# Attention of two layers: another order of score units, row units, value products and transposes

## The reference, cut to what matters

```python
scores = jnp.einsum('bqhd,bkhd->bhqk', q, k) * scale
mask = jnp.tril(jnp.ones((n, n), bool))
scores = jnp.where(mask, scores, -jnp.inf)
attn = jax.nn.softmax(scores, axis=-1)
out = jnp.einsum('bhqk,bkhd->bqhd', attn, v).reshape(b, n, d)
```

## Time and profile before

| | us |
|---|---|
| median of 3 runs (lowest, highest) | 1048.63 (1046.24, 1048.93) |
| profiled execution, own time | 1044.79 |
| its span, first to last instruction | 1043.1 |
| mean granted PE clock | 0.837 |
| busy: PE, DVE, ACT, POOL | 862.9, 605.0, 459.4, 288.2 |
| l0 attention, first row matmul to last copy | 306.3 to 471.3 |
| l1 attention, the same | 747.9 to 913.4 |

### The profile page before, as it was taken

How to read it: one execution, slowest core, us unless ns; L and a number is a source line. 1 busy time by engine, 2 the same in 40 slices (tenths; PEclk the granted TensorE clock), 3 DMA queues, 4 the chain that set the end, 5 groups by cost and what they waited for, 6 DMA issues and landing times. The chain is left out here.

```text
span 1043.1 us, 22638 instructions
## 1 busy us (share of the span) xinstructions
PE 862.9 (83%) x8503; PEld 611.2 (59%) x8503; DVE 605.0 (58%) x2052; ACT 459.4 (44%) x1082; POOL 288.2 (28%) x538
## 2 busy tenths in 40 slices
PE   6874914899968999998999889969889999987884
PEld 3542913777746666657886345534466666576462
DVE  1874695465547878746343634450278878475264
ACT  2573511000003666663232876463246766655054
POOL 0770311355532333330001300000023333340635
PEclk9996556655557999999788999878879999998788
DMA  5055453513210263002000000000000000092461
GB/s 124 1 116 115 123 176 119 108 38 81 55 37 2 50 177 63 2 2 91 1 1 23 6 0 1 1 0 1 1 1 2 2 3 2 2 237 84 173 255 49
DMA packets 54437, 60.48 MB, mean 58 GB/s; under 512 B 9050, under 2 KB 40248, under 8 KB 54073
## 3 DMA queue, kind: packets, MB, share of 16 engines
q1 hardware_dynamic: 43976, 44.31, 15.8%
q10 hardware_dynamic: 7488, 6.85, 2.5%
q0 software_dynamic: 2864, 7.89, 2.2%
HBM read 29.75 MB, written 25.99 MB: 53 GB/s over the span
## 5 line engine op out<-in xcount | busy, mean ns | idle before, releaser
L837 DVE CUSTOM_DVE_ANT_0 l_masked_scores<-psum,mask_q_rows 128x128 bf16<-128x128 f32 (+3 forms) x512 | 220.0, 488 | 60.2 <-PE psum L776 60.2
L854 ACT ACTIVATE l_probs<-psum 128x512 f32<-128x512 f32 (+1 forms) x384 | 171.7, 530 | 75.9 <-PE psum L762 75.8
L868 POOL TENSOR_SCALAR_AFFINE_SELECT l_probs<-l_probs 128x256 f32<-128x256 f32 x256 | 101.5, 409 | 358.1 <-ACT l_probs L854 352.8
L776 PE MATMUL psum<-kb_heads,q_heads 32*128 32x384 f32 (+3 forms) x512 | 93.5, 488 | 10.4 <-DVE l_neg_max_rows L828 8.7
L776 PE MATMUL psum<-l_k_heads,l_q_heads 32*128 32x384 f32 (+3 forms) x512 | 93.8, 492 | 4.4 <-DVE l_neg_max_rows L828 2.7
L762 PE MATMUL psum<-l_q_and_max,l_k_heads 32*128 32x384 f32 (+3 forms) x512 | 91.6, 462 | 0.0
L762 PE MATMUL psum<-l_q_and_max,kb_heads 32*128 32x384 f32 (+3 forms) x512 | 90.9, 457 | 0.0
L796 PE MATMUL psum<-l_probs,rows_32k 128*32 128x256 f32 (+1 forms) x1536 | 82.5, 347 | 1.1 <-POOL l_probs L868 1.1
L776 PEld LDWEIGHTS psum<-kb_heads,q_heads 32*128 32x128 f32 x512 | 58.9, 197 | 18.0 <-DVE l_neg_max_rows L828 8.9
L641 POOL TENSOR_TENSOR v_new_and_ones<-v_and_k_rows 32x128 f32<-32x128 f32 x128 | 54.9, 446 | 49.1 <-DVE v_and_k_rows L618 45.5
L776 PEld LDWEIGHTS psum<-l_k_heads,l_q_heads 32*128 32x128 f32 x512 | 59.5, 198 | 12.0 <-DVE l_neg_max_rows L837 3.9
(11 more groups left out here) (351 smaller groups left out, 1684.7 us busy)
## 6 DMA issues: line engine op xcount, KB each, us to landing
sorted_scratch<-l1p_zeros SPq DMA_DIRECT2D x23, 257.0 KB, 7.1
gram_scratch<-rows_32k SPq DMA_DIRECT2D x4, 1024.0 KB, 5.2
rows_32k<-v_new_and_ones SPq DMA_DIRECT2D x64, 64.0 KB, 2.6
x_rows<-in_L_attn_x_dram SPq DMA_DIRECT2D x16, 128.0 KB, 6.7
heads_scratch<-rows_32k SPq DMA_DIRECT2D x2, 1024.0 KB, 5.4
heads_scratch<-q_kb_T SPq DMA_DIRECT2D x2, 1024.0 KB, 6.0
inverse_scratch<-block_inv SPq DMA_DIRECT2D x2, 1024.0 KB, 4.0
q_heads<-heads_scratch SPq DMA_DIRECT2D x2, 1024.0 KB, 7.0
```

Of the source, the lines that this page charges most:

```text
L776: mm = nc.tensor.matmul(ps[:, row_bank(G, u, i), o:o + w], QT(b, gq)[r, t * P:(t + 1) * P], KT(b, gq)[r, 0:w], start=True, stop=True)
L837: last = nc.vector.tensor_tensor_reduce(out=junk[:, n % 4, o:o + w], in0=ps[:, row_bank(G, u, i), o:o + w], in1=g.maskq[:, N - w:N], scale ...
L854: nc.scalar.activation(PT[:, G % 2, 2 * (u % 2) + i, o:o + w], ps[:, e_bank(G, u, i), 0:w], ACT.Exp, scale=SCALE).then_inc(x_ok, 1)
L868: last = nc.gpsimd.affine_select(out=d, in_=d, pattern=[[0, 2], [1, P]], compare_op=ALU.is_ge, fill=0.0, base=0, channel_multiplier=-1)
```

## The change

Three tables of order change, and all that counts by position in them. Nothing is computed otherwise, and no instruction is added or taken away.

```diff
-PV_TURNS = [(1, 0, 256), (3, 256, 512)]
+SCORE_ORDER = [4, 3, 2, 5, 0, 1]
+ROW_SEQ = [2, 5, 4, 1, 0, 3]
+PV_TURNS = [(2, 0, 256), (5, 256, 512)]
 LEAD = 9
 MAXT_AT = 3
-PV_NEEDS = [max(u for u in range(UNITS) for kb, _ in KEYS[u // 2] if kb * P < q1) + 1 for _, q0, q1 in PV_TURNS]
+SCORE_POS = {u: i for i, u in enumerate(SCORE_ORDER)}
+PV_NEEDS = [max(SCORE_POS[u] for u in range(UNITS) for kb, _ in KEYS[u // 2] if kb * P < q1) + 1 for _, q0, q1 in PV_TURNS]
...
-    return [(n // UNITS, n % UNITS)] if n < UNITS * NGRP else []
+    return [(n // UNITS, ROW_SEQ[n % UNITS])] if n < UNITS * NGRP else []
...
-            SCORE_AT[_G, _k, _i] = len(SCORE_AT)
+            SCORE_AT[_G, SCORE_ORDER[_k], _i] = len(SCORE_AT)
...
-                pe.wait_ge(row_ok, max(ROW_AT[G, UNITS, 0] - 3, ROW_AT[G, UNITS - 1, 1] + 1))
+                pe.wait_ge(row_ok, max(ROW_AT[G, UNITS, 0] - 3, ROW_AT[G, ROW_SEQ[-1], 1] + 1))
...
-                    step([(G, k)], row_unit(LEAD + UNITS * G + k))
+                    step([(G, SCORE_ORDER[k])], row_unit(LEAD + UNITS * G + k))
...
-                    act.wait_ge(e_ps, 2 * UNITS * G + 2 * u + i + 1)
-                    if u == 0 and i == 0 and G >= 2:
+                    act.wait_ge(e_ps, 2 * UNITS * G + 2 * SCORE_POS[u] + i + 1)
+                    if u == SCORE_ORDER[0] and i == 0 and G >= 2:
...
-                for u in range(UNITS):
+                for u in SCORE_ORDER:
```

More of the change, by code:

```diff
@@ L674 @@
 PT_AT = [0, 512, 1024, 896]
-PV_TURNS = [(1, 0, 256), (3, 256, 512)]
+SCORE_ORDER = [4, 3, 2, 5, 0, 1]
+ROW_SEQ = [2, 5, 4, 1, 0, 3]
+PV_TURNS = [(2, 0, 256), (5, 256, 512)]
 LEAD = 9
 MAXT_AT = 3
-PV_NEEDS = [max(u for u in range(UNITS) for kb, _ in KEYS[u // 2] if kb * P < q1) + 1 for _, q0, q1 in PV_TURNS]
+SCORE_POS = {u: i for i, u in enumerate(SCORE_ORDER)}
+PV_NEEDS = [max(SCORE_POS[u] for u in range(UNITS) for kb, _ in KEYS[u // 2] if kb * P < q1) + 1 for _, q0, q1 in PV_TURNS]
 def row_unit(n):
-    return [(n // UNITS, n % UNITS)] if n < UNITS * NGRP else []
-SCORE_AT, ROW_AT, UNIT_AT = {}, {}, {}
+    return [(n // UNITS, ROW_SEQ[n % UNITS])] if n < UNITS * NGRP else []
+SCORE_AT, ROW_AT = {}, {}
 for _n in range(LEAD):
     for _i in range(2):
-        ROW_AT[_n // UNITS, _n % UNITS, _i] = len(ROW_AT)
+        ROW_AT[_n // UNITS, ROW_SEQ[_n % UNITS], _i] = len(ROW_AT)
     if _n == UNITS - 1:
@@ L755, in scoresT @@
                         pe.wait_ge(x_ok, SCORE_AT[G, u, i] - 3)
-                    if u == 0 and i == 0:
+                    if u == SCORE_ORDER[0] and i == 0:
                         pe.wait_ge(row_ok, ROW_AT[G, UNITS, 0] + 1)
@@ L770, in rows @@
                         pe.wait_ge(row_ok, ROW_AT[G, u, i] - 3)
-                    if streamed and u == 0 and i == 0 and gq == 0:
+                    if streamed and u == ROW_SEQ[0] and i == 0 and gq == 0:
                         pe.wait_ge(g.heads_ld[b], 16 * (5 if b else 6))
```

## The result

| | before | after |
|---|---|---|
| median, first comparison (4 and 4 runs) | 1047.43 | 1020.8 (1015.75 to 1023.54) |
| ratio and 95% interval | | 0.976 (0.972 to 0.980) |
| median, second comparison, another chip (17 and 6 runs) | 1043.97 | 1017.67 |
| ratio and 95% interval | | 0.973 (0.968 to 0.977) |
| profiled execution, span | 1044.79, 1043.1 | 1020.33, 1018.6 |

The forecast was 1020.2. Here are the stages of the profile after that answer to the earlier trace rows: the lead to maxT(0), to maxT(1), to maxT(2), the 13 turns, and the tail of layer 0; then one turn, which answers to the earlier trace rows; last the 13 turns of layer 1. The columns are those of the earlier trace rows, and behind PEclk stand the DMA share and GB/s.

The account below looks back on a forecast made before the run. No engine is full; the order of waits in a closed PE and DVE loop sets the 9.27 us turn. Each phase gains 13 x 0.94 + 2.0 = 14.2, both 28.4, from 1048.63 to 1020.2 us; 8-in-10 range 1012 to 1031.

Parts of the forecast that it names:

- The turn: One steady loop turn of the attention, from step A to the next A: 8.33 us, 0.94 less than 9.27.
- The added switch: On PE, one more switch between kinds of matmul in each turn, costed at 0.20 us.
- maxT's wait: PE's wait for DVE before maxT in each turn: 0.11 us instead of 0.71.
- The chain: What sets the 8.33 us turn: A, B up to R0, DVE's R0 and R3, maxT, E, F, pv1.
- pv0's cover: pv0's wait for all six units is hidden by 2.5 us of pv1 and steps A to C.
- Ends of a phase: Start and tail of each attention: 2.0 us gained at the start (bounds 0 and 3), 0 at the tail.
- The sum: Both attentions: 13 x 0.94 + 2.0 = 14.2 us gained in each, 28.4 together, so 1020.2 on the runs' scale.
- Rival 1: PE's busy time is real, so a turn gains at most 0.51 us; time 1033; chance 0.09.
- the rule: Trainium skill page: matmul busy time is no measure of headroom, weight-load busy time is better; it names DVE here (81%).
- Rival 2: No wait left: PE's 7.92 us sets the turn; time 1010; chance 0.04.
- Rival 3: Nothing won: a wait on the critical chain (pv1's exp or R4's bank) returns in full; time 1048; chance 0.04.
- Rival 4: Slower: PE at 1.2 GHz in part of the steady loop; 1058 with 6 such turns; chance 0.04.

Follow-up runs that it names:

- split_maxT: Changed kernel, but only maxT's fourth transpose waits for R3 half 1, the three others go when the bank is free; 1017.27 us, 8.36 a turn.
- short_reads: Changed kernel, but DVE reads only 256 of the 512 columns of R0 and R3; 1009.43 us in a single run, 8.36 a turn.
- pool_4us: Changed kernel with eight extra memsets on POOL in front of the masks of S1 in each group; 1102.42 us, 10.32 a turn.
- turns_only: Kernel before with only the value products moved (pv0 behind the third step, pv1 behind the sixth), old unit orders; 1061.76 us, 9.82 a turn.
- short_both: Changed kernel with R0 and R3 reads cut to 256 columns, and QM too from the third group on; 1013.93 us, 8.28 a turn.
- orders_only: Kernel before with the new orders of score and row units, value products left where they were; 1098.43 us, 10.78 a turn.

## Why the prediction was right

- **The turn.** 8.36 for 8.33, and every station of the turn within 0.03. The terms were durations of the trace of before at the same clock, and the two waits that decide (R3 half 1 on R1's bank, maxT on the last read of R3) came where they had been put. The added switch cost what it had been given.
- **maxT's wait.** 0.71 became about 0.1, as forecast (maxT at 4.18, where PE by the working would have been at 4.06). In split_maxT, where the first transposes don't wait, the way from A to maxT is 4.09 in place of 4.18, which confirms the 0.1. The 0.71 went because pv1 covers R5' and R4', and pv0 covers R3. DVE is idle 0.83 a turn (8.36 less 7.53), where the listed gaps came to 1.05, and no gap is over 0.5.
- **The chain.** Half right. It sets the turn, but a second one of nearly the same length runs over R2', QM and the bank of R4' half 1. The working had that slack as 0.10, and short_reads and split_maxT show that it is gone as soon as maxT comes 0.1 earlier. It was none even in after, as the weight load shown with short_reads tells. Anyone who had taken the prediction's chain as the only one would have promised a gain for either.
- **pv0's cover.** 2.5 forecast, 2.6 to 2.7 by pool_4us.
- **Ends of a phase.** 2.0 a phase forecast; measured 1.7 and 2.2 without the tail, and the tail 0, as taken. The inner split was wrong. The lead and the first round gained 2.0 and 2.5, more than the 1.7 of the narrower first unit, and "the turn behind maxT(1) loses a little wait too" went the other way: 8.23 for 7.93, 0.30 longer. maxT(2) had its 0.71 of wait before too, but this turn has no pv1 yet, under which DVE could work off R5' and R4'. After the change the row halves are held for DVE's reads instead (in three places, 1.0 us), and DVE is busy 7.30 of 8.22 us. So the 2.0 came out about right by errors that cancel: that is luck.
- **The sum.** 28.4 forecast. 27.5 arrived in the phases, and 26.6 and 26.3 in the medians of the two comparisons. That 1020.8 is only 0.6 from the forecast 1020.2 is in part luck too, since the four runs go from 1015.75 to 1023.54.
- **Rival 1 and the rule.** In turns_only PE is busy 9.81 of 9.81, in after 8.34 of 8.36, for the same matmuls. So PE's busy time grows with the waits between them, and the 0.51 a turn that rival 1 derived from it was no bound: 0.91 came. The Trainium skill's page "Perfetto Trace Analysis", section "Identifying the Most-Contended Engine", has matmul busy time as a bad measure of the distance to the limit, and these runs agree. The page says that pipelined instructions look smaller in the trace; here the busy time is larger than the work (9.81 for a sum of 7.92). Its other measure, the busy share of weight loads, doesn't tell these kernels apart well either: 6.41 of 9.81 (65%) against 5.79 of 8.36 (69%).
- **Rival 2** was excluded by DVE's chain, as argued; even short_both stays at 8.28, over 7.92. **Rival 3** did not occur: R4's bank was the tight place that it named, and cost hundredths. **Rival 4** did not occur in after (1.00 in all turns), but in pool_4us, where PE waits 1.89 us in each turn, pieces of the steady loop do run at 0.50.

## What to carry to other kernels

Write one turn of the loop out as a list of starts on each engine, with durations from the trace, and move the order until no engine is late: here that hit each start listed above to 0.03 us, while the busy shares said little. A long stretch of PE in which it feeds nobody (pv1) belongs behind the steps that give the reader the most to do, and narrow units belong in a step with narrow ones. Parts of an order can't be judged one at a time: the value products alone and the two orders alone were slower here, pv0 alone a little faster, and together they gave 0.91 a turn. A half needs its bank some 0.11 us ahead of its turn here, since its weights are loaded only once the bank is free; and when a chain is shortened, look for the second one before promising a gain.

## What was not expected of the hardware

- A half that starts only some 0.04 us late still costs 0.10 us more, its first pass starting anew. In step B of after, the first half starts at 417.68 and a row half at 417.72, and that one's second pass comes at 418.25: 0.53 behind, not the 0.43 of a pass of 512. The weight loads of the two halves show the difference:

```profile
417.46 0.18 PEld L779 LDWEIGHTS psum<-kb_heads,q_heads 32*128 32x128 f32 x1
...
417.72 0.18 PEld L779 LDWEIGHTS psum<-kb_heads,q_heads 32*128 32x128 f32 x1
...
417.83 0.18 PEld L779 LDWEIGHTS psum<-kb_heads,q_heads 32*128 32x128 f32 x1
```

  The half that was in time had its weights loaded from 417.46 on, 0.21 ahead of its first pass; the held one from 417.72, with the pass, and its next load follows 0.11 later. The Trainium skill's page "TensorE: Matmul & The Clock Gate", section "LDWEIGHTS (loading the stationary operand)", has a weight load as its columns over 1.2 in ns, by which 128 columns are an estimated 107 ns. The rows agree in size (0.11 between the loads, 0.10 lost). That the load is the whole reason for the 0.10 is argued, not shown by an experiment.
- The clock in a steady loop: 1.00 in all turns of orders_only, with 0.96 us of PE idle in a turn of 10.79, but pieces at 0.50 in pool_4us, with 1.89 idle in a turn of 10.32.
